# A three-stage decoder layer on one core: the normalised and transposed x made by VectorE from a transposed copy in DRAM, and PSUM banks given out anew

## What is computed

```python
x = x + attn(layernorm(x), Wq, Wk, Wv, Wff, bff)            # "A": softmax(q k^T) v, 16 heads
x = x + xattn(ctx, ctx, layernorm(x), ...)                  # "X"
h = layernorm(x)                                            # "F": scores, top 8, gate
x = x_after_X + h + gate * sum_k(w_k * aux_values[idx_k])   # "G": the weighted sum of gathered rows
```

## Time and profile before

| | |
|---|---|
| median of 3 executions | 2862.33 us (2860.9 to 2866.07) |
| the profiled execution | 2859.07 us, its span 2857.2 us |
| TensorE busy | 2649.0 us, 93% of the span |
| VectorE busy | 2104.9 us, 74% |
| ScalarE busy | 1421.1 us, 50% |
| GpSimd busy | 785.7 us, 27% |
| TensorE in the chain of work that ended last | 90% |
| DMA, mean | 110 GB/s |

### The profile page before, as it was taken

The page is one execution under the profiler, slowest core; times in us unless marked ns, Lnnn a source line. Parts: engine busy times, 40 slices in busy tenths (PEclk is TensorE's granted clock), DMA queues, the critical chain, the costliest instruction groups (busy, mean ns, idle before and its releaser), DMA issues.

```text
span 2857.2 us, 53958 instructions
## 1 busy us (share of the span) xinstructions
PE 2649.0 (93%) x18042; PEld 1983.5 (69%) x18042; DVE 2104.9 (74%) x4071; ACT 1421.1 (50%) x4214; POOL 785.7 (27%) x651
## 2 busy tenths in 40 slices
PE   6899999999999999999999999999999999999830
PEld 4667777777777777777777777777777777777610
DVE  4446778878777788877777878777788877777652
ACT  2345554445455444555554445455544455555343
POOL 0001323222223232222323222223232222233245
PEclk9999999999999999999999999999999999999965
DMA  5112323333333332333323333333332333333799
GB/s 167 57 57 76 103 91 118 103 102 105 107 101 100 102 120 86 108 107 109 103 91 116 110 96 104 107 101 104 99 120 89 107 107 110 101 93 108 180 237 181
DMA packets 102683, 313.05 MB, mean 110 GB/s; under 512 B 14577, under 2 KB 15089, under 8 KB 94417
## 3 DMA queue, kind: packets, MB, share of 16 engines
q1 hardware_dynamic: 54002, 180.37, 19.2%
q0 software_dynamic: 48640, 132.16, 17.4%
HBM read 269.35 MB, written 43.12 MB: 109 GB/s over the span
## 4 chain that ended last, share of the span: by engine, by line
PE 90%; issue 2%; DVE 2%; DMA 2%; ACT 1%; POOL 1%; SPq 1%; POOLq 0%; DVEq 0%; ACTq 0%
PE psX L985 45%; PE psA L985 19%; PE psF L985 8%; PE psA L994 8%; PE psA L1072 4%; PE psA L1049 4%; PE psX L994 3%; DMA vg<-in_L_ffn_aux_values,idx 1%; DVE xT_lo L775 1%; PE psF L994 1%; ACT xT_hi L567 1%; POOL out L540 1%; POOL vg L523 0%; SPq L371 0%; ACT paT L550 0%
## 5 line engine op out<-in xcount | busy, mean ns | idle before, releaser
L523 POOL DMA_INDIRECT vg<-in_L_ffn_aux_values,idx x512 | 516.5, 1009 | 1635.1 <-DVE agg L890 830.9
L586 ACT ACTIVATE pa<-psA,nmax 112x224 f32<-112x224 f32 x1024 | 443.6, 449 | 150.3 <-DVE nmax L794 147.6
L890 DVE SCALAR_TENSOR_TENSOR agg<-vg,wt,agg 112x512 f32<-112x512 f32 x420 | 367.5, 875 | 16.2 <-DMA vg<-in_L_ffn_aux_values,idx 2.9
L794 DVE TENSOR_REDUCE nmax<-psA 112x4 f32<-112x896 f32 x256 | 266.7, 1083 | 149.8 <-PE psA L1049 149.8
L985 PE MATMUL psX<-big,gT 128*112 128x375 f32 x1024 | 333.4, 478 | 1.3 <-ACT nx L622 1.0
L985 PE MATMUL psX<-pT,cx 125*128 125x224 f32 x1536 | 307.5, 357 | 0.0
L550 ACT COPY paT<-psA 112x448 f32<-112x448 f32 x512 | 236.5, 544 | 111.1 <-PE psA L994 108.7
L985 PEld LDWEIGHTS psX<-pT,cx 125*128 125x128 f32 x1536 | 285.5, 190 | 7.7 <-issue 0.3
L807 DVE TENSOR_TENSOR pa<-pa,rsum 112x896 f32<-112x896 f32 x256 | 279.5, 1092 | 8.8
L985 PEld LDWEIGHTS psX<-big,gT 128*112 128x112 f32 x1024 | 177.4, 176 | 127.1 <-ACT nx L622 1.2
L985 PE MATMUL psX<-m,xnxT 128*112 128x512 f32 x512 | 235.6, 603 | 0.0
(11 more groups left out here) (195 smaller groups left out, 5301.5 us busy)
## 6 DMA issues: line engine op xcount, KB each, us to landing
big<-in_ctx_t SPq DMA_DIRECT2D x32, 1500.0 KB, 6.7
cx<-in_ctx SPq DMA_DIRECT2D x32, 1500.0 KB
xa<-in_x SPq DMA_DIRECT2D x32, 448.0 KB, 4.7
xr<-in_x SPq DMA_DIRECT2D x32, 448.0 KB, 3.9
out<-x SPq DMA_DIRECT2D x32, 448.0 KB, 3.1
agg_scratch<-agg SPq DMA_DIRECT2D x60, 224.0 KB, 6.4
vg<-in_L_ffn_aux_values,idx POOLq DMA_INDIRECT x512, 3.7
over_weights<-agg_scratch SPq DMA_DIRECT2D x15, 448.0 KB, 13.5
```

What stands on the lines that cost most here:

```text
L523: pool.indirect_dma_start(vg[:, c % SLOTS, k, :], None, aux_values, bass.IndirectOffsetOnAxis(ap=idx[:, t, n:n + 1], axis=0))\
L586: last = nc.scalar.activation(pa[:, t, h, :], psA[0:R, h, t * S:(t + 1) * S], ACT.Exp, bias=nmax[:, k % 2, h, t:t + 1], accum_out=rsum[:, ...
L794: nc.vector.tensor_reduce(nmax[:, k % 2, h:h + 2, :], psA[0:R, h:h + 2, 0:T * S].rearrange("p h (t s) -> p h t s", t=T), AX_X, ALU.max, ne ...
L890: last = nc.vector.scalar_tensor_tensor(dst, vg[:, c % SLOTS, k, :], w, dst, ALU.mult, ALU.add)
```

## The change

x comes a second time, transposed on the host to [batch, 128, 4*224] (x_t). A new stream N works one batch ahead of A. N norm: VectorE takes the statistics of xa and writes mean and 1/sqrt to `moments`; SyncE stores these 448 numbers to DRAM. N spread: SyncE loads them back, broadcast to all 128 partitions. N center: VectorE subtracts the mean from x_t and multiplies it (128x896, in SBUF), ScalarE casts all of it to xT_hi, VectorE writes xT_lo. A norm and A turn are gone. The value product has four jobs of 256 columns. The mixes of A go to ring psF, whose count runs two batches behind A (LAG), with the jobs that are absent at the start and the end made up by TensorE's own signals (`catch_up`). The setup products use the two banks of psX. ORDER is new, turn 30 is unrolled too, and the first steps of batch 0 stand in a list FIRST.

```diff
 ORDER = (
-    ("A", "norm", 0), ("X", "enter", 0), ("A", "turn", 0), ("G", "sum", 0), ("X", "norm", 0), ("A", "qk", 0),
-    ("A", "value", 0), ("X", "turn", 0), ("G", "sum", 1), ("A", "score", 0), ("G", "sum", 2), ("X", "query", 0),
-    ("A", "share", 0), ("F", "norm", 0), ("A", "prob", 0), ("A", "qk", 1), ("A", "qk", 2), ("G", "sum", 3),
...
-    ("F", "top", 0), ("F", "score", 2), ("A", "share", 3), ("A", "mix", 2), ("X", "out", 0), ("G", "sum", 7),
-    ("A", "prob", 3), ("F", "score", 3), ("F", "top", 1), ("A", "mix", 3), ("X", "out", 1),
+    ("A", "qk", 0), ("G", "sum", 0), ("G", "sum", 1), ("X", "enter", 0), ("X", "norm", 0), ("A", "value", 0),
+    ("X", "turn", 0), ("G", "sum", 2), ("A", "score", 0), ("A", "share", 0), ("X", "query", 0), ("A", "prob", 0),
+    ("F", "norm", 0), ("A", "qk", 1), ("G", "sum", 3), ("A", "qk", 2), ("F", "turn", 0), ("X", "score", 0),
+    ("A", "score", 1), ("N", "norm", 0), ("G", "sum", 4), ("F", "route", 0), ("X", "score", 1), ("A", "mix", 0),
+    ("A", "share", 1), ("A", "qk", 3), ("F", "learn", 0), ("X", "prob", 0), ("A", "prob", 1), ("F", "score", 0),
+    ("G", "sum", 5), ("X", "prob", 1), ("A", "score", 2), ("X", "mix", 0), ("G", "sum", 6), ("A", "share", 2),
+    ("N", "spread", 0), ("A", "mix", 1), ("A", "prob", 2), ("F", "score", 1), ("G", "sum", 7), ("A", "score", 3),
+    ("X", "mix", 1), ("F", "top", 0), ("A", "mix", 2), ("F", "score", 2), ("A", "share", 3), ("X", "out", 0),
+    ("A", "prob", 3), ("N", "center", 0), ("F", "score", 3), ("X", "out", 1), ("A", "mix", 3), ("F", "top", 1),
 )
-FILLS = {("A", "turn"): 2, ("A", "qk"): 1, ("A", "value"): 2, ("A", "score"): HB, ("A", "prob"): 2 * T,
+FILLS = {("A", "qk"): 1, ("A", "value"): 2 * T, ("A", "score"): HB, ("A", "prob"): 2 * T,
...
+FIRST = (("N", "norm", 0), ("N", "spread", 0), ("W", "split", 0), ("N", "center", 0), ("W", "split", 1),
+         ("W", "split", 2), ("W", "keys", 0), ("W", "keys", 1), ("W", "keys", 2), ("W", "keys", 3))
+SETUP = {1: (("W", "route", 0), ("W", "m2", 0)),
+         2: (("W", "m2", 1), ("W", "m2", 2), ("W", "m2", 3), ("W", "router", 0)),
+         7: (("W", "cb", 0), ("W", "m1", 0), ("W", "m1", 1)),
+         12: (("W", "m1", 2), ("W", "m1", 3), ("W", "gb", 0))}
+RING = {("A", "mix"): "F"}
...
         def spare(n):
-            return (psX, psF)[n // 2 % 2][:, n % 2, :]
+            return psX[:, n % 2, :]
...
-            return jobs[s] // banks[s] * b + j // banks[s]
+            return jobs[s] // banks[s] * (b + LAG if s == "F" else b) + j // banks[s]
...
-                batch = {"A": i, "X": i - 1, "F": i - 2, "G": i - 3, "W": 0}
+                batch = {"N": i + 1, "A": i, "X": i - 1, "F": i - 2, "G": i - 3, "W": 0}
...
+            for s, name, arg in FIRST:
+                if (s, name) in step:
+                    step[s, name](0, arg)
...
-            with eng.Fori(3, B - 1) as i:
+            with eng.Fori(3, B - 2) as i:
                 iteration(i)
+            iteration(B - 2)
             iteration(B - 1)
...
             sp.dma_start(xa[:, :, :], tiles(row(x, 0))).then_inc(x_loaded, 16)
+            sp.dma_start(flat(centered), row(x_t, 0)).then_inc(xt_loaded, 16)
...
+            def store_moments(b, _):
+                sp.wait_ge(moments_ready, b + 1)
+                with nc.allow_non_contiguous_dma(reason="448 numbers"):
+                    sp.dma_start(row(moments_dram, b).rearrange("k r -> r k"),
+                                 moments[:, :, :].rearrange("p k t -> p (k t)")).then_inc(moments_stored, 16)
+                if not (isinstance(b, int) and b == B - 1):
+                    sp.dma_start(xa[:, :, :], tiles(row(x, b + 1))).then_inc(x_loaded, 16)
+
+            def spread_moments(b, _):
+                sp.wait_ge(moments_stored, 16 * (b + 1))
+                wait(sp, xt_scaled, b)
+                sp.dma_start(flat(spread), row(moments_dram, b).rearrange("k r -> (k r)").partition_broadcast(P))\
+                    .then_inc(moments_spread, 16)
+
+            def next_xt(b, _):
                 if isinstance(b, int) and b == B - 1:
                     return
-                wait_full(sp, "A", FILL["A", "turn", 0] + 1, b)
-                sp.dma_start(xa[:, :, :], tiles(row(x, b + 1))).then_inc(x_loaded, 16)
+                sp.wait_ge(xT_split, b + 1)
+                sp.dma_start(flat(centered), row(x_t, b + 1)).then_inc(xt_loaded, 16)
...
+            def center_hi(b, _):
+
+                act.wait_ge(xt_scaled, b + 1)
+                wait_full(act, "A", max(FILL["A", "value", 0] + 2 * T - 1, FILL["A", "qk", NB - 1]), b - 1)
+                nc.scalar.copy(xT[0][:, :, :], centered[:, :, :]).then_inc(xT_hi, 1)
...
+            def x_moments(b, _):
                 dve.wait_ge(x_loaded, 16 * (b + 1))
-                norm("A", b, xa, xa, xa_normed)
+                statistics("N", b, xa, rstd["N"][:, :])
+                assert count["N"] == N_STEPS
+                wait(dve, moments_stored, 16 * b)
+                nc.vector.tensor_copy(moments[:, 0, :], mv["N"][:, :, 0])
+                nc.vector.tensor_copy(moments[:, 1, :], rstd["N"][:, :]).then_inc(moments_ready, 1)
...
+            def center_scaled(b):
+                mean, rstd = (spread[:, k, :].unsqueeze(1).to_broadcast([P, C, S]) for k in range(2))
+                xt = centered[:, :, :]
+                dve.wait_ge(xt_loaded, 16 * (b + 1))
+                dve.wait_ge(moments_spread, 16 * (b + 1))
+                nc.vector.tensor_tensor(xt, xt, mean, ALU.subtract).then_inc(mean_taken, 1)
+                dve.wait_ge(mean_taken, b + 1)
+                nc.vector.tensor_tensor(xt, xt, rstd, ALU.mult).then_inc(xt_scaled, 1)
+
+            def center_lo(b, _):
+                center_scaled(b)
+                dve.wait_ge(xT_hi, b + 1)
+                lo(xT[1][:, :, :], centered[:, :, :], xT[0][:, :, :]).then_inc(xT_split, 1)
...
+            def catch_up(b, j):
+
+                while isinstance(b, int) and absent and absent[0] < (b, j):
+                    at, job = absent.pop(0)
+                    wait_free(pe, "F", job, at)
+                    pe.sem_inc(full["F"][job % banks["F"]], 1)
+                    pe.sem_inc(drained["F"][job % banks["F"]], 1)
...
-                wait_drained(pe, "A", FILL["A", "turn", 0] + 1, b)
-                for t in range(T):
-                    j = FILL["A", "value", 0] + t
-                    wait_free(pe, "A", j, b)
-                    filled("A", j, product3(bank("A", j)[0:R, :], [(both(xT, ALL, c, slice(t * R, (t + 1) * R)),
-                                                                    both(wvT, ALL, c, ALL)) for c in range(C)]))
+                pe.wait_ge(xT_split, b + 1)
+                for t in range(T):
+                    for half in range(2):
+                        j, cols = FILL["A", "value", 0] + 2 * t + half, slice(half * D // 2, (half + 1) * D // 2)
+                        wait_free(pe, "A", j, b)
+                        filled("A", j, product3(bank("A", j)[0:R, 0:D // 2],
+                                                [(both(xT, ALL, c, slice(t * R, (t + 1) * R)), both(wvT, ALL, c, cols))
+                                                 for c in range(C)]))
...
-                wait_free(pe, "A", j, b)
+                wait_free(pe, "F", j, b - LAG)
...
-                wait(pe, setup_drained, fills[0] - 3)
+                wait(pe, setup_drained, fills[0] - 1)
```

More of the change, by code:

```diff
@@ L112, with plan @@
          ("F", "turn"): 2, ("F", "route"): 1, ("F", "learn"): 1, ("F", "score"): 2}
-SETUP = {("A", "norm"): (("W", "split", 0),),
[5 rows of a table removed]
[L119 to L124, removed]
-assert all(JOBS[_s] % BANKS[_s] == 0 for _s in JOBS)
-A_STEPS, X_STEPS, F_STEPS, G_STEPS = 21, 15, 18, 12
+FIRST = (("N", "norm", 0), ("N", "spread", 0), ("W", "split", 0), ("N", "center", 0), ("W", "split", 1),
+         ("W", "split", 2), ("W", "keys", 0), ("W", "keys", 1), ("W", "keys", 2), ("W", "keys", 3))
+SETUP = {1: (("W", "route", 0), ("W", "m2", 0)),
[3 rows of a table added]
+RING = {("A", "mix"): "F"}
+def plan(order):
+    fill, jobs = {}, {"A": 0, "X": 0, "F": 0}
+    for s, step, arg in order:
+        if (s, step) in FILLS:
+            ring = RING.get((s, step), s)
+            fill[s, step, arg] = jobs[ring]
+            jobs[ring] += FILLS[s, step]
+    assert all(jobs[s] % BANKS[s] == 0 for s in jobs)
+    return fill, jobs
+FILL, JOBS = plan(ORDER)
+N_STEPS, A_STEPS, X_STEPS, F_STEPS, G_STEPS = 13, 8, 15, 18, 12
+LAG = 2
 def build(nc, x, ctx, attn_wq_t, attn_wk_t, attn_wv_t, attn_wff_t, attn_bff, x_wk, x_wv, x_bv, x_wq, x_bq,
           x_wo_t, x_bo, q_proj_w, router_w_t, aux_keys_t, aux_values, mask, unc_w1_t, unc_b1, unc_w2,
-          unc_b2, gate_w1, gate_bias, ctx_t, out):
+          unc_b2, gate_w1, gate_bias, ctx_t, x_t, out):
     stack = ExitStack()
@@ L478, in _ @@
                           ("W", "cb"): first_cxT, ("W", "gb"): first_ctx,
```

(21 more changed lines are left out.)

124 lines of the change are left out of this document (71 added, 53 removed), and 9 rows, old and new, of tables (ORDER, SETUP).

## The result

The changed kernel takes **3038.71 us** (median of 4 executions, 3035.11 to 3041.45), the kernel before 2863.77 beside it: ratio 1.0611 [1.0592, 1.0629], **6.1% slower**. Forecast were 2841 us and a range that ends at 2880. The profiled execution has a span of 3038.0 us, 180.8 more than before.

What follows compares the result with a forecast made beforehand. TensorE, 98% busy, was taken to bound each turn. From the profiled 2859.07 us, -45 for the turns, +21 for the start and +3 for batch 0 gave 2838, or 2841 us as median; range 2805 to 2880.

Steps and rivals of the forecast that it cites:

- The transposes and their wait: TensorE's eight transposes of xa and its wait for xT_lo in each turn were to vanish: -2.40 us a turn.
- The value halves: Value product as 48 matmuls of 256 columns for 24 of 512: 0 us a turn, up to +0.46.
- rival 2: Centring itself late, so A qk 0 and later steps wait: a turn gives +0.1 to +0.5 us, 2890 us; slower chance 0.23.
- X turn: TensorE's step after the value product, waiting for VectorE's late X norm: a new stall of 0.2 us a turn.
- prob 0: TensorE was to wait for VectorE's second share half, late because G sum 2 meets GpSimd's addition: 0.8 us a turn.
- the rest of the turn holds: Later in the turn, shares 1 and 2 come when needed or up to 0.9 us early; no further stall.
- a price in the start: Storing the moments before batch 0 was to keep SyncE's queue 4.1 us and land at about 28 us.
- -1.4 us a turn: Net of a full loop turn: -2.40 for transposes and wait, 0, +1.0 for two stalls; 40.6 us over batches 3 to 31.
- The start: First A qk 0 moves from 26.3 to 47 us behind the moments' DRAM round trip: +21 us, bounds 17 and 27.
- the turns of batches 0 to 2: Batch 0's turn +3 us, bounds 0 and 6; batches 1 and 2 without stalls, 2 x 2.4 us gained.
- The last turn and the end: Same list, only bookkeeping of the absent mixes added: 0, up to 1 us.
- Rival 1: Cover holds in the loop, VectorE's slack hides the stalls: a turn gives 2.3 us, 2815 us in all; chance 0.25.

Runs made afterwards that it cites:

- sums_later: Changed kernel with 16-byte moment stores, G sum 6 after A share 2, N center last in FIRST, G sums 1 and 2 after A score 0 and A share 0: 2836.19 us.
- g4_before_norm: Changed kernel with G sum 4 moved ahead of N norm in ORDER: 2958.23 us, ratio 1.0333 to the kernel before.

## Why the prediction was wrong

**What held.** The transposes and their wait, -2.40 us: gone. The value halves: 116 ns forecast (the line through its two rows gives 115), 117.5 measured, so 0 was the right end of the range. The centring is not late (rival 2): its passes over 128x896 take 1.09 us each as costed, it ends 1.7 us before A qk 0 wants it, and the four gathers that GpSimd issues from 1257.50 to 1261.37 don't slow it. X turn was to stall 0.2 us and stalls 0.28; prob 0 0.8 and stalls 0.70.

**The step that failed** is one sentence: "By these rows the rest of the turn holds: share 1 and share 2 come at the moment they are needed or up to 0.9 us early". I had laid out VectorE's queue by durations alone. G sum 6 stands in it ahead of share 2, and a G sum waits for a gather; that wait I took as zero because it was none before. It is 4.0 us. Its cause lay in a term that I costed only once: the store of 448 numbers had a price in the start, where it delays the broadcast, and none in the loop, where I said only that the broadcast "is issued behind the ctx_t load some 25 us before". Who shares the DMA engines with it in those microseconds, the gathers among others, I did not ask. This is no rival of mine: the slower case that I priced, the centring, is another mechanism.

**Its size.** Forecast -1.4 us a turn, measured +5.4, a difference of 6.8: 3.5 for the wait, 2.7 for the clock behind it, and 0.6 for smaller ones. The clock's part I hadn't either; for the start I had counted the lower clock after a long idle time, for the loop no such idle time.

**The start.** TensorE and VectorE there, and SyncE's queue:

```profile
46.37 3.76 PE L1046 MATMUL psX<-sc,gT 128*112 128x512 f32 x4 [23.36 <-DVE wffT L977]
49.14 1.18 PE L1046 MATMUL psA<-xT_hi,wqT_hi 128*128 128x224 f32 x1
```

```profile
36.29 1.09 DVE L834 TENSOR_TENSOR centered<-centered,spread 128x896 f32<-128x896 f32 x1 [21.47 <-DMA spread<-moments_scratch]
```

```profile
21.58 0.46 SPq L461 DMA_DIRECT2D moments_scratch<-moments  x1
22.08 0.49 SPq L464 DMA_DIRECT2D xa<-in_x  x1
31.83 0.35 SPq L469 DMA_DIRECT2D spread<-moments_scratch  x1
```

and in the kernel before, just ahead of the load of the earlier trace rows from which I took the store's price:

```profile
10.04 1.07 SPq L371 DMA_DIRECT2D bvc<-in_L_xattn_bv  x1
```

A qk 0 starts at 49.1, forecast 47, before 26.3: +22.9 for +21. The shape was another than I wrote: the queue lets go of the store after 0.46 us (I had 4.1), but it lands 10 us later (I had 3), and 31.83 stands where I had 28. Two errors of opposite sign, and it is luck that their sum is small. The 4.1 us had no ground even in the trace before: bvc has 512 elements of 4 bytes like bqc, and kept the queue 1.07 us where bqc kept it 4.66. Had I looked for the store's price in its landing and in what moves beside it, the loop would have followed.

**The whole account**, to A qk 0 of batch 3 and on, in us of difference. At batch 3 it starts at 301.47 for 282.58, +18.9; but X enter (7.0) of that turn now comes behind it, so +25.9 for equal work, of which 22.9 is the start and 3.0 the turns of batches 0 to 2 (forecast 3 - 3 x 2.4 = -4.2, most of the difference in batch 0's turn, where TensorE waits 11.2 us for shares and waited 5.5 before). At batch 31 it starts at 2757.19 for 2588.16, +169.0: 28 turns cost 150.1 (forecast -39). The last turn and the end cost 4.8 (forecast 1). Sum 22.9 + 3.0 + 150.1 + 4.8 = 180.8, the whole difference of the spans. The loop holds 189 of the 202 us by which the forecast of the span failed.

**Rival 1** (2815 us, 2.3 us a turn) no run reaches. sums_later comes nearer to the forecast itself: with the gathers out of the way a turn gains 82.35 - 80.7 = 1.65 us, where the forecast was 1.4. A gain of this size was there to be had, but not with this ORDER and this store together.

## What to carry to other kernels

A step costs its waits as well as its durations: when a queue is laid out by durations, write beside each step what else releases it, a gather above all, and set the steps whose input comes by DMA behind those that the busiest engine waits for. A DMA of many tiny pieces is priced twice, once for who waits for it and once for every transfer that runs beside it. And a wait on a matmul-bound path can cost more than itself: here 3.51 us of it brought 2.7 us more by the slower clock behind it, and 1.57 us brought none.

## What the hardware showed that I had not expected

- 448 stores of 4 bytes keep other transfers of the core under 100 GB/s for 8.5 us; 112 stores of 16 bytes, with the same 1.8 KB, let them run after 3.6.
- The queue of SyncE is free of such a store after 0.3 to 0.5 us; in the earlier trace rows a load of 512 such elements kept it 4.66 us. The number of elements doesn't decide this: the load bvc, with as many elements, kept it 1.07 us just before, and in the changed kernel the two loads kept it 5.17 and 2.15 us. What stood ahead of each may be the reason; that wasn't tried.
- After 3.51 us without a matmul the granted clock was 0.50 for the next 3.5 us and 0.59 for the 3.5 after, with TensorE busy; after 1.57 us it stayed at 1.00. 48 needless matmuls in between made a turn 1.9 us shorter.
- The same loop code started an instruction of VectorE 0.9 us later in one kernel than in another whose only difference stands ahead of the loop, and in one whose only difference is in TensorE's list; the cause is open.
- Beside an addition of GpSimd over 112x1024, a VectorE instruction on 112x2 took 2.92 us in place of 0.16 and ended with it (1201.25 and 1201.23, g4_before_norm).
